# Self-attention of a diffusion block on one core: units of two, by query halves, with a lead of 14 units

## The reference

```python
qkv = x_norm @ W_qkv + b_qkv
q, k, v = jnp.split(qkv, 3, axis=-1)          # 16 heads of 16 channels
attn_w = jax.nn.softmax(jnp.einsum('bhqd,bhkd->bhqk', q, k) * scale, axis=-1)
attn_out = jnp.einsum('bhqk,bhkd->bhqd', attn_w, v)
```

## Time and profile before

| | us |
|---|---|
| median of 3 runs | 1603.7 (1603.05 to 1605.82) |
| profiled execution | 1601.8 |
| its span | 1600.0 |
| PE, DVE, ACT, POOL busy | 1490.6, 1050.8, 769.6, 377.6 |
| query maxima (DVE, L2251), 256 | 310.5 |
| exponentials (ACT, L1640), 512 | 276.8 |
| key products (PE, L999), 512 | 188.5 |
| query products (PE, L984), 512 | 186.7 |
| values (PE, L1011), 2048 | 158.7 |
| fillers (PE, L591), 382 | 119.8 |

### The profile page before, as it was taken

One profiled execution on the slowest core, in us unless ns is written; L12 is line 12 of the kernel. 1 busy time (PEld: TensorE's weight loads), 2 busy tenths in 40 slices (PEclk: granted clock), 3 DMA queues, 4 the chain that ended last, 5 costly groups with the idle time before them and its releaser, 6 DMA issues.

```text
span 1600.0 us, 26614 instructions
## 1 busy us (share of the span) xinstructions
PE 1490.6 (93%) x10593; PEld 937.2 (59%) x10593; DVE 1050.8 (66%) x2960; ACT 769.6 (48%) x1232; POOL 377.6 (24%) x419
## 2 busy tenths in 40 slices
PE   5899999999999999987999999999999999998898
PEld 3457765444355857656765767544445475765676
DVE  2574456999537446899457535599972745579963
ACT  1335421788844533325543543168885363333454
POOL 4420006342125110114133000634210701001330
PEclk9999999999999999999999999999999999999999
DMA  9500037121020000000130001812102000000000
GB/s 339 164 0 1 0 112 106 21 42 22 2 79 1 1 0 3 2 1 1 46 125 1 1 1 61 157 22 36 27 2 79 1 1 1 2 2 1 1 1 27
DMA packets 37663, 59.81 MB, mean 37 GB/s; under 512 B 7347, under 2 KB 27091, under 8 KB 36643
## 3 DMA queue, kind: packets, MB, share of 16 engines
q1 hardware_dynamic: 25239, 34.71, 6.6%
q0 software_dynamic: 9520, 16.04, 6.2%
q10 hardware_dynamic: 2780, 7.36, 1.3%
HBM read 42.22 MB, written 2.10 MB: 28 GB/s over the span
## 4 chain that ended last, share of the span: by engine, by line
PE 66%; DVE 21%; issue 6%; ACT 3%; DMA 1%; POOL 1%; ACTq 0%; DVEq 0%; POOLq 0%
PE ps L999 10%; PE ps L1011 9%; PE ps L463 5%; PE ps L1321 4%; PE ps L984 3%; PE ps L591 3%; PE ps L1112 3%; DVE taken L2384 3%; DVE rs L2062 3%; PE ps L1346 2%; PE ps L1103 2%; DVE taken L2396 2%; DVE mxw L2054 2%; PE ps L1173 2%; PE ps L599 2%
## 5 line engine op out<-in xcount | busy, mean ns | idle before, releaser
L2251 DVE TENSOR_REDUCE mm<-ps 128x1 f32<-128x1024 f32 x256 | 310.5, 1223 | 35.1 <-PE ps L984 31.7
L1640 ACT ACTIVATE pt<-ps 128x512 f32<-128x512 f32 x512 | 276.8, 600 | 61.0 <-PE ps L999 43.6
L2502 POOL TENSOR_TENSOR rstd<-ve,minus_half 128x4 f32<-128x4 f32 x32 | 34.9, 1091 | 695.3 <-DVE ve L1926 695.3
L999 PE MATMUL ps<-qx,kx 64*128 64x512 f32 x512 | 188.5, 445 | 1.0 <-ACT pt L1640 1.0
L984 PE MATMUL ps<-kx,qx 48*128 48x512 f32 x512 | 186.7, 444 | 0.2
L1011 PE MATMUL ps<-pt,v 128*32 128x256 f32 x2048 | 158.7, 390 | 0.0
L999 PEld LDWEIGHTS ps<-qx,kx 64*128 64x128 f32 x512 | 79.0, 184 | 95.9 <-ACT pt L1640 85.9
L591 PE MATMUL ps<-filler 128*128 128x512 f32 x382 | 119.8, 440 | 0.0
L2139 DVE TENSOR_TENSOR rlo<-ring,rhi 128x512 fp32r<-128x512 f32 x48 | 33.2, 691 | 91.9 <-ACT ring L1590 91.9
L1011 PEld LDWEIGHTS ps<-pt,v 128*32 128x32 f32 x2048 | 42.9, 108 | 85.5 <-ACT pt L1640 61.3
L984 PEld LDWEIGHTS ps<-kx,qx 48*128 48x128 f32 x512 | 75.4, 185 | 24.4 <-issue 19.3
(11 more groups left out here) (374 smaller groups left out, 3319.7 us busy)
## 6 DMA issues: line engine op xcount, KB each, us to landing
wm<-in_L_xcond_W_mlp_dram SPq DMA_DIRECT2D x4, 1024.0 KB, 8.6
qx<-q_hi POOLq DMA_DIRECT2D x64, 64.0 KB, 2.5
kx<-k_hi POOLq DMA_DIRECT2D x64, 64.0 KB, 2.5
w3a<-in_L_xcond_w_m_dram SPq DMA_DIRECT2D x2, 2048.0 KB, 7.6
w<-in_L_xcond_e_w_dram SPq DMA_DIRECT2D x6, 512.0 KB, 7.9
w<-in_L_xcond_e_w_dram SPq DMA_DIRECT2D x2, 1536.0 KB, 12.8
s_ada<-in_L_xcond_w_ada_dram ACTq DMA_DIRECT2D x1, 2304.0 KB, 23.3
qx<-q_lo POOLq DMA_DIRECT2D x32, 64.0 KB, 2.4
```

The lines of the kernel that those rows point to most:

```text
L999: pe.matmul(ps[:, bank, :], kx[r, p % 4, kc * P:(kc + 1) * P], qx[r, p % 4, half * 512:(half + 1) * 512], start=True, stop=True).then_inc( ...
L1640: act.activation(pt[:, u % 8, half * 512:(half + 1) * 512], ps[:, bank, :], ACT.Exp, scale=QK_SCALE).then_inc(st_read, 1)
L2251: return dve.tensor_reduce(mm[:, p % 2, e, t:t + 1], place(), X, ALU.max).then_inc(ring_read, 1)
```

## The change

The lead is 14 units. The scores by keys go by query halves: units 0 to 7 of a pair treat the first 512 queries, 8 to 15 the others; the two products of a unit are two chunks of 128 keys. The maxima are turned and sent per half (two turns per pair, two row DMAs each). PE's loop takes two units at a time: four key products with four query products among them, then both bursts of the two units before. When the queries have ended, the four key products come as one chunk of either unit, then the other. `weigh_values` takes the 512 columns of one chunk.

The queries start earlier: the first four units use only the first halves of queries and keys of pair 0, which POOL now sends as separate DMAs as soon as each part is ready; k comes before q in the second halves. The values of the second half and the second eight heads' products (`full_step`) are spread among the lead units, in the place of fillers. POOL waits for the fills ahead of the first maxima rows. The rounding copies of the second eight heads go from ACT to POOL, behind the first maxima rows of pair 1, and the later spreads are cut into a query and a key part. On DVE one low part stands ahead of a normalisation.

```diff
-LEAD = 22
+LEAD = 14
...
+def keys_of(n):
+
+    if n < 0:
         return ()
+    return tuple((n + j, i) for j in range(2) for i in range(2)) if n + LEAD < UNITS else tuple((n + j, i) for i in range(2) for j in range(2))
...
-                keep_busy(6, 9)
+                full_step(0)
+                full_step(1)
                 ln(2, 1)
-                keep_busy(6, 4)
+                full_step(2)
...
+                def key_scores(p, u, i):
+
+                    half, e, kc = u // T, u % 2, 2 * (u % T // 2) + i
...
+                def weigh_values(w, i):
+
+
+                    p, half, kc = w // T, w % T // TB, 2 * (w % TB) + i
                     pe.wait_ge(st_read, b * N_KEY + entry_of[2 * w + 1])
+                    if kc == 0 and half == 0 and p >= 1:
                         pe.wait_ge(acc_read, b * NP + p)
                     for e in range(2):
+                        weights = pt[:, (2 * w + e) % 8, i * BLK:(i + 1) * BLK].rearrange("p (j a c) -> p j a c", a=2, c=P)
+                        for part in range(2):
+                            o = 32 * (2 * e + part)
+                            ins = pe.matmul(ps[o:o + 32, 7, half * 2 * P:(half + 1) * 2 * P], v2[:, kc, VS * (2 * p + e):VS * (2 * p + e) + 32],
+                                            weights[:, :, part, :], start=kc == 0 and half == 0, stop=kc == T - 1 and half == 1)
...
+                linear(take() + 1, wqk2, KC, hT[:, 1], (hT_ready, b * 2 * N_HT + 10)).then_inc(ring_ready, 1)
+                linear(take() + 1, wqk2, 0, hT[:, 1]).then_inc(ring_ready, 1)
                 full_step(3)
                 pe.wait_ge(v2_clear, b + 1)
-                keep_busy(7, 7)
-                for n in range(-LEAD, UNITS):
...
+
+                def queries(m):
+
+                    q, at_m = divmod(m, 2 * T)
+                    if m == 0:
+                        pe.wait_ge(first_ld, b * N_FIRST + N_SPR)
+                    elif m == TB:
+                        pe.wait_ge(first_ld, b * N_FIRST + N_FIRST)
+                    elif m == T:
+                        pe.wait_ge(spread_ld[0], b * (first + 2 * N_SPR) + first)
+                    elif at_m == 0:
+                        pe.wait_ge(spread_ld[q % 3], loads[q])
+                    query_scores(q, at_m)
+
+                for m in range(LEAD):
+                    if m == 12:
+                        pe.wait_ge(full_ready, b * 4 + 4)
+                    if m >= 12:
+                        keep_busy(5, 2)
+                    queries(m)
+                    if m < TB:
+                        values(1, (m,))
...
+                        turn_maxima(0, 0)
+                    elif m == 11:
+                        pe.wait_ge(full_ready, b * 4 + 3)
...
+                        ins.then_inc(gates_spread, 1)
+                pe.wait_ge(fill_ld, b * 64 + 64)
+                pe.wait_ge(gates_ready, b + 1)
+                for n in range(0, UNITS, 2):
                     (p, u), m = divmod(n, 2 * T), n + LEAD
                     q, at_m = divmod(m, 2 * T)
-                    if m == 2 * T:
-                        pe.wait_ge(gates_ready, b + 1)
-                    if n >= 0:
-                        if n == 0:
-                            pe.wait_ge(fill_ld, b * 64 + 64)
-                        if u == 0:
-                            pe.wait_ge(mrow_ld[p % 2], b * N_MROW * NP // 2 + N_MROW * (p // 2 + 1))
-                        key_scores(p, u, 0)
-                    if m == 4:
-                        pe.wait_ge(full_ready, b * 2 + 1)
-                    if m >= 4 and n < 4:
-                        keep_busy(4 if m < 2 * T else 7, 3 if n < 0 else 1)
+                    if u % T == 0:
+                        pe.wait_ge(mrow_ld[u // T], (b * NP + p + 1) * N_MROW)
+                    if n == 0:
+                        keep_busy(7, 1)
                     if m < UNITS:
-                        if at_m == 0:
-                            pe.wait_ge(spread_ld[q % 4], b * 2 * N_SPR + N_SPR * (q // 4 + 1))
-                        query_scores(q, at_m)
-                    if m < 4:
-                        full_step(m + 4)
...
-                    if n >= 0:
-                        key_scores(p, u, 1)
-                    for i in bursts_of(n):
-                        weigh_values(i // 2, i % 2)
-                    if at_m == 1 and 1 <= q <= NP:
-                        turn_maxima(q - 1)
-                    if u == 13 and p >= 1:
+                        for j in range(2):
+                            key_scores(p, u + j, 0)
+                            queries(m + j)
+                            key_scores(p, u + j, 1)
+                    else:
+                        for i in range(2):
+                            for j in range(2):
+                                key_scores(p, u + j, i)
+                    if n >= 2:
+                        for i in range(2):
+                            weigh_values(n // 2 - 1, i)
+                    if at_m == T and q < NP:
+                        turn_maxima(q, 0)
+                    elif at_m == 0 and 1 <= q <= NP:
+                        turn_maxima(q - 1, 1)
+                    if u == 12 and p >= 1:
                         finish(p - 1)
...
-                act.wait_ge(full_ready, b * 2 + 2)
-                for i in range(4):
-                    act.wait_ge(spread_ld[i], b * 2 * N_SPR + N_SPR)
-                for qk in range(2):
-                    act.activation(dense[2 * qk][:, :], full[qk], ACT.Copy).then_inc(hi_ready, 1)
...
+                    for unit, i in keys_of(n):
+                        probabilities(unit, i)
+                    if at_m == T and q < NP:
+                        maximum_rows(0)
+                    elif at_m == 0 and 1 <= q <= NP:
+                        maximum_rows(1)
...
+                low_part(0, 0, 0).then_inc(lo_ready, 1)
...
+                def maximum_rows(p, half):
...
+                    for e in range(2):
+                        r = 64 * e + 3 * HD
+                        pool.dma_start(qx[r:r + 2, p % 4, half * BLK:(half + 1) * BLK].rearrange("r (t c) -> r t c", c=P), mxT[T * e:T * (e + 1), half, :]).then_inc(mrow_ld[half], 16)
...
+                low, high = slice(0, BLK), slice(BLK, L)
+                pool.wait_ge(hi_ready, b * 6 + 1)
+                pool.sem_inc(passed, 1)
+                part(0, 0, 0, low, first_ld)
+                ln(2, (1,))
+                pool.wait_ge(hi_ready, b * 6 + 2)
+                part(1, 0, 0, low, first_ld)
...
-                for p in range(3):
-                    spread(p)
+                pool.wait_ge(lo_ready, b * 4 + 1)
+                part(0, 1, 0, low, first_ld)
+                pool.wait_ge(lo_ready, b * 4 + 2)
+                part(1, 1, 0, low, first_ld)
+                pool.wait_ge(first_ld, b * N_FIRST + N_SPR)
+                pool.wait_ge(hi_ready, b * 6 + 3)
+                pool.sem_inc(passed, 1)
+                part(1, 0, 0, high, first_ld)
+                pool.wait_ge(ring_read, b * N_RING + 1)
+                part(1, 1, 0, high, first_ld)
+                pool.wait_ge(hi_ready, b * 6 + 4)
+                part(0, 0, 0, high, spread_ld[0])
+                pool.wait_ge(ring_read, b * N_RING + 2)
+                part(0, 1, 0, high, spread_ld[0])
+                spread(1)
                 pool.wait_ge(v_done, b * NB + NB)
                 pool.sem_inc(passed, 1)
                 for i, wide in enumerate((qx, kx)):
                     for e in range(2):
                         pool.dma_start(wide[64 * e + 3 * HD:64 * e + KA, :, :], g["c_fill"][i]).then_inc(fill_ld, 16)
-                spread(3)
+                pool.wait_ge(fill_ld, b * 64 + 64)
                 for p in range(NP):
-                    maximum_rows(p)
+                    maximum_rows(p, 0)
                     if p == 0:
+                        spread(2)
+                    elif p == 1:
...
                         for qk in range(2):
+                            pool.tensor_copy(dense[2 * qk][:, :], full[qk]).then_inc(hi_ready, 1)
                             pool.wait_ge(hi_ready, b * 6 + 4 + qk + 1)
                             pool.tensor_tensor(dense[2 * qk + 1][:, :], full[qk], dense[2 * qk][:, :].bitcast(F32), ALU.subtract).then_inc(lo_ready, 1)
-                    if p >= 1 and p + 3 < NP:
-                        spread(p + 3)
+                    elif p + 3 < NP:
+                        spread(p + 3, (0,))
+                    maximum_rows(p, 1)
+                    if p == 0:
+                        spread(3)
+                    elif p == 1:
+                        spread(4)
+                    elif p + 3 < NP:
+                        spread(p + 3, (1,))
```

More of the change, by code:

```diff
@@ L1068, in _ @@
+                    if at_m == T and q < NP:
[3 more added lines that the diff above has]
+                    if u == 12 and p >= 1:
                         finish(p - 1)
[L1069 to L1071 removed]
+                for i in range(2):
```

(11 more changed lines are left out.)

252 lines of the change are left out of this document (128 added, 124 removed).

## The result

The changed kernel takes 1594.7 us, the kernel before 1604.8 beside it: a ratio of 0.9931, 95% interval 0.9909 to 0.9952. It is faster, as forecast, and inside the range, but by 10 us instead of 22. The profiled execution took 1591.3 us, span 1589.4 (before: 1600.0).

A forecast was written before the change was run, and what follows sets the result against it. PE's own sequence was taken to bound the mixed stage, DVE 5% behind. Lead -18.6 and key loop +7.8 make -10.8 us per sample, -21.6 for both, from 1603.7: 1582 us, range 1549 to 1604.

The forecast's parts named there:

- The step: Mixed stage and tail: two units take 2.64 us against 2.46, the fourth key waiting for the first one's bank.
- The turn: Key loop: turning maxima on PE, fifteen behind a first key at 0.28 us each, 4.2 us.
- the finish: Key loop: seven finishes on PE at 0.66 us each, 4.6 us.
- The hidden wait: Rival, key loop: fourth key finds its bank free, DVE sets 2.51 us per step; 1547 us, chance 0.20.
- The key loop: First key to last value, per sample: 177.8 us against 170.0, +7.8 us.
- The lead: Before the mixed stage: 14 units instead of 22, started earlier, bring the first key to 264.7, 18.6 us earlier.
- PE's chain: Lead: products start at 240.5 and fourteen units at about 1.5 us end at 261.5.
- POOL's chain: Lead: DMAs and fills issued by 254.8, fills landed 262.1, maxima rows landed 264.7, setting the first key.
- late lead-in: Rival, lead: first key at 270, 5.3 us per sample less gain; 1592 us, chance 0.10.
- The clock: Rival, near first key and norm's last transposes: idle PE drops to half clock for 3.4 us stretches; 1584 to 1589, chance 0.12.
- What costs nothing: Moved low part on DVE, rounding copies on POOL (6.7 us) and maxima rows' way were to add no time.
- the rows' margin: Key loop: maxima rows take 3.9 us of the 5.3 us before the key needing them, 1.4 us spare.

The follow-up runs named there:

- e3: The changed kernel with the key loop's units taken one at a time, bursts placed as in the kernel before: 1587.1 us.
- e9: The changed kernel with two fillers ahead of each of the first twelve lead units and 13 more in the gap before the first key: 1589.8 us.
- e12: The changed kernel with small first fills, the other slots' fills behind the second maxima rows, 12 fillers in the lead and seven in the gap: 1583.4 us.
- e1: The changed kernel with only the first of four slots filled ahead of the first maxima rows, the others right behind them: 10.1 us less than the change.
- e6: The kernel before without the three fillers in each unit of its lead (54 fillers), nothing else changed: slower than the kernel before, time not given in the text.
- e8: The changed kernel with a lead of 12 units instead of 14: 2 us above the expected 1625 to 1631 us.
- e2: The changed kernel with 27 fillers between the last lead query and the wait for the fills: 1592.6 us.
- e13: As e12, but with the key loop's units taken one at a time: 4.6 us below e12.
- e4: The changed kernel with the edits of e1 and e3 together, fills by slot and units one at a time: 1575.4 us.
- e11: The changed kernel, units in twos, with e1's fills, one filler in each of the first twelve lead units and seven in the gap: 1584 us or more.

## Why the prediction was half right

**The bound.** Right: PE's own sequence sets the mixed stage, with units in twos and in ones (e3: PE busy in all of 63.87 us, VectorE in 61.44).

**The step.** Forecast 2.64, measured 2.61, by the mechanism that was given: the fourth key behind the first exponential. The turn costs 0.21 instead of 0.28, the finish 0.59 (441.06 to 441.65) instead of 0.66: the forecast took the durations of the earlier trace rows, but the next product starts before they end, in the kernel before too (319.43 to 319.64, 322.11 to 322.69). A pair is 21.98; the forecast's numbers made 8 x 2.64 + 2 x 0.28 + 0.66 = 22.3. The hidden wait, the rival with the highest chance, did not come.

**The key loop.** Forecast +7.8, measured +7.7 and +8.2: a match by luck. At full clock (e9, e12) it is +5.7 to +7.1; the shorter step and turns would have given 2 us more, and the half clock took them.

**The lead.** PE's chain, forecast to end at 261.5, ended at 259.65. POOL's chain reached the end of its fills at 254.9, forecast 254.8, by two errors that cancel: it began 1.0 us later, and an issue took 0.48 us instead of 0.51. Then the step that failed: "The fills land after 4.6 to 9.9 us, median 7.3: 262.1". POOL waits for all four, so the last landing counts, not the median of four. It took 9.7 us here, and 9.9 in the earlier trace rows. The row had the right number; with it the sum is 254.8 + 9.9 + 1.04 + 1.6 = 267.3, 0.4 us from the measured 267.71, and the forecast 1587. No term of the sum held the one filler between the rows and the first key, which took 0.69 us at half clock (267.02 to 267.71). The measured key lies nearer to the 270 of the rival "late lead-in", which had 0.10 of the chance, than to 264.7.

A page of the Trainium skill would have misled here as well: "DMA: Bandwidth & Descriptors", section "Anatomy of one DMA — SWDGE (gpsimd) path", fits a transfer issued by POOL as about 2 us plus its bytes at 436 GB/s. For one of these fills that makes an estimate of 2.6 us, for one of 64 KB 2.2. The small fills of e1 come near it (2.5 us measured); the four large ones, issued in a row, do not (5.0 to 9.7).

**The second sample** was taken as a repetition. Its lead was 1.2 us longer (27.9 against 26.7); the first fill was issued 13.0 us after the first query instead of 11.9, behind a pause of 1.02 us of POOL at 1009.3 for which the trace names no cause. Its first query itself came 0.7 us later behind its values (22.2 us instead of 21.5). The time 1033 that the forecast gave for its first key also left out what the first sample gains.

**The clock.** Named as a rival, with 0.12 and 1584 to 1589 alone, for falls of 3.4 us, but put at nothing in the sum. It fell for 13.65 us in each sample and cost 4.4 us of loop in both (e9; 4.9 by the medians). What was underrated is that the lead's fillers were there for it: "22 units, a pair of query products and mostly three fillers each" was read as slack that sets the pace, and e6 shows that these fillers hold the clock for 34 us. The Trainium skill's page "TensorE: Matmul & The Clock Gate" has a section "A second HAM failure mode: psum-queue depth-cycling", on a clock that goes back and forth because of many small idle times between groups of matmuls. e6 agrees in that its clock fell with no gap over 0.99 us, but it then stayed down for 34 us.

**What costs nothing.** Right: no wait of PE for rows behind the first key in the change; the copies on POOL (two of 1.05 and two of 2.4 us, 6.9 in all) moved nothing; and the rows' margin is near what was worked out (e8: 1.7 instead of 1.4 us).

**The sum.** By the rows, the 11 us are 3.05 and 4.85 us of later first keys, 0.3 us of loop, and 2.8 us in the rest. In each sample 2.4 to 2.5 us come from the last landing instead of the median and 0.7 from the filler at half clock; the second sample adds its later first query and longer lead. The clock's 4.4 us of loop are hidden by the cheaper step, turn and finish (about 4 us). The rest changes from run to run: the same work takes 218.7 to 223.0 us from the start to the first product that makes v, 534.5 to 537.8 from the first sample's last value matmul to the second's first product that makes v, and 379.1 to 382.4 from the last value matmul to the end in the sixteen traces, and the runs of one kernel mostly differ by 2 to 8 us. So these 2.8 us are not shown to come from the change.

**Still open.** Why the clock fell at 257.2 in one sample of e2 and at 260.6 in the change with the same work ahead of it; and why it fell in the first steps of e13 and not of e12, with PE busy in both. The half turns and the order of the keys by query halves were in all kernels with the short lead, and were not tried alone.

## What to carry to other kernels

A wait for several transfers ends with the last one, so take the longest landing of the row and not its median, and ask what else stands on that queue: moving a large transfer out of one small transfer's way may put it into the next one's. Fillers that look like slack may be holding TensorE's clock; before they are removed or a gap is opened, cost the stretch behind them at half speed, and if they are kept, keep them without a gap up to the work they protect. When a change has several parts, try each part alone: here the earlier lead won 29 us in both samples, and a loop that is 16 us longer, by units in twos, more turns and the clock, gave half of it back.

## What the hardware showed unexpectedly

- The clock stayed low while PE worked: 0.50 for 34.05 us with PE busy in 30.95 of them (e6), and for 20.5 us in e4 with PE busy in all of them.
- At half clock a filler takes 0.79 us (e6) instead of 0.49 at the same place in the kernel before, and two bursts 1.93 instead of 1.07 (e2).
- Transfers issued by POOL can land late behind earlier ones of its queue: 4 KB landed after 1.7 us, and after 7.2 to 7.8 us behind 768 KB of fills (e11).
